# Order of the last gap and the first loads, engine of the low parts, and unread TensorE matmuls, in a layer of attention and gated feed-forward

## The chip, the cores and the metric

One core of one Trainium2 chip runs the whole program. The metric is the device time of one launch, in microseconds.

## What is computed

The input is x, 4 x 1024 x 256 in fp32. The layer is attention with 16 query heads and 4 key and value heads of width 16 (rotary positions, full softmax over 1024 keys), output projection, residual and layer norm; then a gated feed-forward of width 1024 with dequantised integer weights, residual and layer norm.

```python
q = rope((x @ wq).reshape(B, S, 16, 16)); k = rope((x @ wk).reshape(B, S, 4, 16)); v = (x @ wv).reshape(B, S, 4, 16)
scores = einsum('bqkgd,bskd->bkgqs', q.reshape(B, S, 4, 4, 16), k) / 4
x = layernorm(x + einsum('bkgqs,bskd->bqkgd', softmax(scores), v).reshape(B, S, 256) @ wo)
x = layernorm(x + (silu(x @ Wg.T) * (x @ Wu.T)) @ Wd.T)      # W = (w_int - 128) * scale
```

## The kernel before

**Stages.** The kernel is one program with an instruction list written by hand for each engine. Stage one projects x in eight blocks m of 512 positions (batch b = m // 2, half c = m % 2). Stage two is the attention, in four pairs of key heads, each of four halves of eight tiles. Stage three is the output projection and the feed-forward, with the norms. Engines wait for each other by semaphores alone.

**A block of stage one.** TensorE makes two q products (j = 0, 1) in plain fp32, each of two matmuls of 128x128 with 512 columns (`project_q`, L1179), and the k and v products (`project_kv`, L1194). VectorE multiplies the q products by cosine and sine (`rotary_q`, L706). GpSimd adds or subtracts these (`rotate`, L539). ScalarE rounds the result to its high part (`high_part`, L970), and the low part is the rest: by GpSimd (`low_of`, L547) or by VectorE (`low_first`, L726). SP stores both to q_parts in device memory (`store_q`, L380). After the second block of a batch VectorE makes the five key products (`rotary_k`, L715 and L719), GpSimd turns them (`rotate_k`, L554), and high and low parts are stored (`store_k`). In the next batch's first block `project_kv` waits for these key products, since they are read from its bank.

**Which engine takes a low part.** For j = 1 it is always GpSimd. For j = 0 it is VectorE in blocks 0 to 4 (`FIRST` is 5) and GpSimd in blocks 5 to 7. In an odd block VectorE's low part stands ahead of its key products.

**The gap.** The softmax needs a bound of the scores for each query. It comes from maxima over keys, for which three arrays are held: keys of the first half, the differences of the halves, and the "gap". TensorE makes the gap of a batch with one fp32 matmul of `key_signs` and the rotated keys (`make_gap`, L1203), ScalarE takes its high part (`gap_high`, L996) and VectorE the rest (`gap_low`, L733). SP stores both (`store_gap`, L391).

**Early work.** After FIRST blocks the maxima of the first halves start between the projections. The table `early[n, h]` says what follows hook h of block n (six hooks a block, and n = 8 after the last block): transposes of V (`transpose_v`, L1157), gaps, maxima (`max_block`, L1138, a matmul of 48 rows with 512 columns; two of a step use different rows and run side by side) and the split of the shift. TensorE, VectorE and ScalarE walk the same table, and from it a list `places` gives each entry a bank of PSUM in turn. Entries of the first kind are cut at zero by ScalarE (`difference`, L1007), and VectorE takes their maximum together with the second kind (`take_max`, L751). With n = 8, hook 1 has the V transposes of batch 3, and hook 5 has the last six steps, twelve maxima, and then the gap of batch 3.

**Loads for it.** `first_loads` on SP waits until blocks 0 and 1, keys and gap of batch 0 are stored, then issues six k_max loads (L324) and four q_sb loads (L314, L315). It stands in block 3, between the x load of block 6 (L336) and `store_q(3, 1)`. TensorE waits for them in `max_loaded(0)`, ahead of the first maxima, hook 0 of block 5.

**Start of the attention.** After the table TensorE goes to `attention`: maxima, scores (L1289) whose first banks must have been read, ScalarE's exponentials (L1062) and the products with V (`pv`, L1231), into pv_bank, which is the same bank as v_bank of stage one.

Of the kernel before, what the change touches and what calls it, by code (L numbers as in the profile page):

```python
# [6 lines left out]
B, S, E = 4, 1024, 256  # L7
# [6 lines left out]
P = 128  # L14
# [22 lines left out]
FIRST = 5  # L37
HOOKS = 6
BLOCKS = 2 * B
WARM = 3  # L40
MIXED = (0, 2, 4, 6)
PER = UNITS * G * S // P
HALVES = UNITS * QH
# [4 lines left out]
TT = CH // P  # L48
# [9 lines left out]
def layer(nc, x, xT, wq, wkv, wo, gate_w, gate_scale, up_w, up_scale, down_w, down_scale,  # L58
          cos, sin_q, cos_k, sin_k, identity, out):
    ctx = ExitStack()  # L60
    with ctx:
        def sb(name, shape, dt=fp32, scope=ctx):
            return scope.enter_context(nc.sbuf_tensor(name, shape, dt))
# [16 lines left out]
        ident = sb("ident", [P, P])  # L80
# [82 lines left out]
        k_bank, v_bank = ring_bank[2], pv_bank  # L163
# [45 lines left out]
        def paired(half, t, r):  # L209

            return KT * half + t < LEAD or (r == 0 and t in MIXED)

# [10 lines left out]
        def step(i):  # L223

            half, t = divmod(i // 2, KT)
            return [(half, 4 * t + 2 * (i % 2) + r) for r in range(GROUPS)]

        early = {(n, h): [] for n in range(BLOCKS + 1) for h in range(HOOKS)}
# [4 lines left out]
        for i in range(2 * LEAD):  # L233
            n, h = divmod(FIRST * HOOKS + i, HOOKS)
# [1 line left out]
            if i == 2 * KT + 1:  # L236
                where.append((0, "split"))
            where.extend(step(i))
        early[BLOCKS, HOOKS - 1].append(("gap", B - 1))
        for n in range(BLOCKS + 1):  # L240
            if n == BLOCKS:
                wide_from = len(readers)
# [30 lines left out]
        def taken_through(key):  # L273

            return ring_used, readers[:places[key] + 1].count("max")
# [41 lines left out]
        def load_k(dst, pair, s, done, queue):  # L317
            parts = QH + 1 if dst is k_max else QH
            head = UNITS * pair + s
            for r in range(GROUPS):  # L320
                for combo, part in enumerate((0, 0, 1)):
                    src = k_parts[head // HKV, part, 0:parts].rearrange("c (d h) t -> d h c t", h=HKV)[:, head % HKV]
                    row = r * GROUP + combo * D
                    queue.dma_start(dst[s][row:row + D].bitcast(fp32).rearrange("d (c t) -> d c t", c=parts), src).then_inc(done[s], 16)  # L324
# [4 lines left out]
        def _(sp):  # L329

            def load_kv(pair, s):
                load_k(k_sb, pair, s, kv_loaded, sp)


            def load_x(m):
                sp.dma_start(x_in[m], xT_v[:, :, m * CH:(m + 1) * CH]).then_inc(x_loaded[m], 16)  # L336
# [56 lines left out]
            def projections(b, first, last):  # L393
                for c in range(2):
                    m = 2 * b + c
                    if last and c == 0:
                        load_kv(0, 0)
                        load_k(k_max, 0, 1, kmax_loaded, sp)
                        load_q(0, QH, sp)
                    store_q(m, 0)  # L400
                    if c == 0 and not first:
                        store_gap(b - 1)
                    if m + 3 < BLOCKS:
                        load_x(m + 3)
                    if m == 3:
                        first_loads()
                    if last and c == 1:
                        load_shift(0, 0, taken_through((0, "split")))
                    store_q(m, 1)
                    if m == 4:  # L410
                        load_q(0, 1, sp)
                    if c == 1:
                        store_k(b)
# [111 lines left out]
        def _(pool):  # L525
# [36 lines left out]
            for m in range(BLOCKS):  # L562
                b, c = divmod(m, 2)
                rotate(m, 0)
                if c == 0 and b:
                    low_of_k(b - 1)
                rotate(m, 1)
                if m >= FIRST:
                    low_of(m, 0)
                low_of(m, 1)  # L570
                if c == 1:
                    rotate_k(b)
# [9 lines left out]
            for n, (w, w_h, w_l) in enumerate(((gate_w, gate_h, gate_l), (up_w, up_h, up_l), (down_w, down_h, down_l))):  # L582
                flat_h, flat_l = (t[:].rearrange("p k n -> p (k n)") for t in (w_h, w_l))
                rows = w.shape[0] // 2
                for half in range(2):
                    i = 2 * n + half
# [102 lines left out]
        def _(dve):  # L689
# [18 lines left out]
            def rotary_k(b):  # L708

                dve.wait_ge(proj_ready, 3 * (2 * b + 1) + 3)  # L710
                if b == 0:
                    dve.wait_ge(k_tables_loaded, 16 * 2)
                else:
                    dve.wait_ge(k_rot_ready, b)
                dve.tensor_tensor(by_cos[2][:], k_bank[:], cosk_sb[:], ALU.mult).then_inc(k_parts_ready, 1)  # L715
                step = HKV * HALF
                for at in range(0, P, 2 * step):
                    for to, src in ((at, at + step), (at + step, at)):
                        dve.tensor_tensor(by_sin[2][to:to + step], k_bank[src:src + step, :], sink_sb[src:src + step, :], ALU.mult).then_inc(k_parts_ready, 1)  # L719

            def low_first(m):
                b, c = divmod(m, 2)
                if b:
                    dve.wait_ge(stored[2 * c], 16 * 2 * b)
                dve.wait_ge(hi_ready, 2 * m + 1)
                dve.tensor_tensor(low[2 * c][:], rotated[0][:], high[2 * c][:].bitcast(fp32), ALU.subtract).then_inc(lo_ready[0], 1)  # L726
# [40 lines left out]
            def early_maxima(n, h):  # L767
                for key in early[n, h]:
                    if key[0] == "v":
                        continue  # L770
                    if key[0] == "gap":
                        gap_low(key[1])
                        continue
                    half, e = key
                    if e == "split":
                        split_shift(entry(key), 0, 0, None)
                        continue
                    take_max(half, e)
                    if e == MAXES - 1:
                        row_maxima(half)  # L780

            for m in range(BLOCKS):
                b, c = divmod(m, 2)
                if m == 1:
                    dve.wait_ge(ident_loaded, 16)
                    dve.tensor_tensor(key_signs[:], ident[:, 0:HKV * D], ident[:, HKV * D:P], ALU.subtract).then_inc(signs_ready, 1)
                early_maxima(m, 0)
                rotary_q(m, 0)
                early_maxima(m, 1)
                early_maxima(m, 2)  # L790
                rotary_q(m, 1)
                early_maxima(m, 3)
                early_maxima(m, 4)
                if m < FIRST:
                    low_first(m)
                if c == 1:
                    rotary_k(b)
                early_maxima(m, 5)
            for h in range(HOOKS):
                early_maxima(BLOCKS, h)  # L800
# [315 lines left out]
        def _(pe):  # L1116

            pe.wait_ge(warm_ready, 1)
            for n in range(WARM):
                pe.matmul(v_bank[:], by_cos[2][:, 0:P], by_cos[2][:], start=True, stop=True)  # L1120
            pe.wait_ge(wq_loaded, 16)

            def free_bank(key):
                pos = places[key]
                before = last_in(bank_index(pos), pos)
                if before is not None:
                    pe.wait_ge(*taken(before))
                elif wide_from <= pos < early_entries:
                    pe.wait_ge(parts_ready, Q_PARTS * BLOCKS)
                return bank_of(key)  # L1130

            def max_block(half, e):
                bank = free_bank((half, e))
                k, t = half % HALVES, e // 4
                qt, i = max_pair(t)
                r, kind = blocks(half, t)[e % 4]
                rows = slice(r * GROUP, r * GROUP + ROWS)
                pe.matmul(bank, q_sb[k][rows, i, qt * P:(qt + 1) * P], k_max[k // QH][rows, kind * CH:(kind + 1) * CH],  # L1138
                          start=True, stop=True).then_inc(ring_ready, 1)
# [13 lines left out]
            def transpose_v(b):  # L1153
# [3 lines left out]
                    ins = pe.transpose(bank[:, t * P:(t + 1) * P], v_rows[b % 2][:, t * P:(t + 1) * P], ident[:])  # L1157
                ins.then_inc(ring_ready, 1)

            def early_work(n, h):  # L1160
                for key in early[n, h]:
                    if key[0] == "v":
                        pe.wait_ge(ident_loaded, 16)
                        transpose_v(key[1])
                    elif key[0] == "gap":
                        make_gap(key[1])
                    elif key[1] == "split":
                        transpose_max(key[0])
                    else:
                        if key[1] == 0:  # L1170
                            max_loaded(key[0])
                        max_block(*key)

            def project_q(m, j, k):
                i = 2 * m + j
# [40 lines left out]
            for h in range(HOOKS):  # L1216
                early_work(BLOCKS, h)

            pe.wait_ge(parts_ready, Q_PARTS * BLOCKS)
            pe.wait_ge(k_parts_ready, K_PARTS * B)  # L1220
            pe.wait_ge(v_rows_ready, B)
# [45 lines left out]
            def attention(p, first, last):  # L1267
                for k in range(HALVES):
                    n = HALVES * p + k
                    s = k // QH  # L1270
                    for t in range(KT):
# [30 lines left out]

                        if t not in MIXED:
                            if split_at(g) is not None:
# [142 lines left out]
```

## Time and profile before

| | us |
|---|---|
| runs before, median (lowest to highest of 3) | 942.2 (941.97 to 942.79) |
| profiled execution, its own time | 944.88 |
| its span, first to last instruction | 943.1 |
| TensorE matmuls busy | 917.6 (97%) |
| VectorE busy | 756.4 (80%) |
| ScalarE busy | 715.4 (76%) |
| GpSimd busy | 247.5 (26%) |
| mean granted TensorE clock | 0.983 of full |

The profile is one execution. Its span lies 1.8 us under that execution's own time. Busy times of TensorE are modelled ends of pipelined matmuls, so full busy time is not peak work; a plain fp32 matmul appears as two records. The granted clock is a share of the full 2.4 GHz. An entry in brackets behind a row is the idle time of the engine just before it and what ended that. The stage of projections is the first tenth of the span; the rest is attention until about 700 us and then the feed-forward.

### The profile page before, as it was taken

What the parts mean: (1) busy time and instruction counts of PE and PEld (TensorE: products, weight loads), DVE (VectorE), ACT (ScalarE), POOL (GpSimd) and SP (SyncE); (2) the same over time, 40 slices, a digit from 0 to 9 for tenths busy, and PEclk for the clock granted to TensorE, in tenths of its full rate; (3) what the DMA queues carried; (4) which work ended last, traced back from release to release, by engine and by line L of the source; (5) the groups of instructions that cost most, each with busy time, mean ns of one, the idle gap of its engine ahead of it and who ended that gap; (6) DMA issues with size and microseconds to landing.
All of it is one profiled execution on the core that took longest, in us unless ns stands there. A gap on an engine that the chain in (4) does not pass through costs nothing.

```text
span 943.1 us, 15754 instructions
## 1 busy us (share of the span) xinstructions
PE 917.6 (97%) x5566; PEld 467.0 (50%) x5566; DVE 756.4 (80%) x1520; ACT 715.4 (76%) x930; POOL 247.5 (26%) x211
## 2 busy tenths in 40 slices
PE   8798999999999999999999999999999999999995
PEld 3233434344344434343434444444435888888884
DVE  5768899999999999999999999999973456655544
ACT  1345888989888898988998889988887555555564
POOL 5643565010001001001000100400101666656454
PEclk9977999999999999999999999999999999999998
DMA  7867533133131332213313123221110201101001
GB/s 251 267 182 191 126 87 94 47 79 76 44 74 43 59 75 69 51 44 75 81 44 70 50 50 81 69 55 42 32 52 15 69 23 46 46 25 43 23 23 47
DMA packets 50080, 68.78 MB, mean 73 GB/s; under 512 B 13520, under 2 KB 23760, under 8 KB 50000
## 3 DMA queue, kind: packets, MB, share of 16 engines
q1 hardware_dynamic: 49136, 64.61, 26.7%
q0 software_dynamic: 864, 3.15, 1.1%
q8 instruction: 46, 0.75, 0.3%
q14 instruction: 34, 0.28, 0.1%
HBM read 46.74 MB, written 16.25 MB: 67 GB/s over the span
## 4 chain that ended last, share of the span: by engine, by line
PE 91%; DVE 2%; ACT 2%; issue 1%; DMA 1%; POOL 1%; SPq 1%; POOLq 0%; DVEq 0%
PE pv_bank L1231 27%; PE ring_bank L1138 26%; PE pair_bank L1289 13%; PE pair_bank L1352 12%; PE pv_bank L1361 3%; PE ring_bank L1361 3%; PE ring_bank L1241 2%; PE pair_bank L1179 1%; ACT probs L1062 1%; PE pair_bank L1138 1%; PE ring_bank L1151 1%; POOL rotated L539 1%; PE ring_bank L1256 1%; DMA q_sb<-q_parts 1%; PE pv_bank L1120 1%
## 5 line engine op out<-in xcount | busy, mean ns | idle before, releaser
L1062 ACT ACTIVATE probs<-pair_bank 128x1024 f32<-128x1024 f32 x512 | 496.4, 1026 | 69.1 <-PE pair_bank L1289 67.7
L754 DVE TENSOR_REDUCE block_max<-ring_bank 128x1 f32<-128x512 f32 x732 | 469.0, 682 | 32.2 <-PE ring_bank L1138 24.2
L1138 PE MATMUL ring_bank<-k_max,q_sb 48*128 48x512 f32 x1004 | 316.0, 478 | 3.6 <-DMA q_sb<-q_parts 2.9
L1231 PE MATMUL pv_bank<-probs,v_all 128*32 128x512 f32 x2048 | 273.7, 606 | 0.6 <-ACT probs L1062 0.5
L1138 PEld LDWEIGHTS ring_bank<-k_max,q_sb 48*128 48x128 f32 x1004 | 137.0, 185 | 252.7 <-DVE block_max L754 126.0
L1289 PE MATMUL pair_bank<-q_sb,k_sb 50*128 50x512 f32 x1024 | 204.7, 416 | 1.7 <-ACT probs L1062 0.9
L617 POOL TENSOR_TENSOR attn<-attn,inv_rows 128x1024 f32<-128x1024 f32 x7 | 16.7, 2382 | 492.3 <-DMA inv_rows<-inv_d 492.3
L1289 PEld LDWEIGHTS pair_bank<-q_sb,k_sb 50*128 50x128 f32 x1024 | 101.5, 187 | 34.1 <-ACT probs L1062 14.2
L919 DVE SCALAR_TENSOR_TENSOR hid<-pair_bank,up_s,silu 128x512 f32<-128x512 f32 x64 | 47.9, 748 | 86.9 <-ACT silu L1102 86.9
L751 DVE CUSTOM_DVE_ANT_0 above<-ring_bank,above 128x512 f32<-128x512 f32 x137 | 94.4, 691 | 15.4 <-PE ring_bank L1138 6.3
L659 POOL TENSOR_TENSOR hid_l<-hid,hid_h 128x512 fp32r<-128x512 f32 x64 | 82.8, 1294 | 86.9 <-ACT hid_h L1088 86.4
L1007 ACT ACTIVATE above<-ring_bank 128x512 f32<-128x512 f32 x135 | 80.6, 599 | 7.3 <-PE ring_bank L1138 3.9
L1102 ACT ACTIVATE silu<-pair_bank,gate_s 128x512 f32<-128x512 f32 x64 | 43.7, 683 | 47.5 <-PE pair_bank L1352 47.5
L1231 PEld LDWEIGHTS pv_bank<-probs,v_all 128*32 128x32 f32 x2048 | 40.4, 108 | 74.2 <-issue 73.4
L1088 ACT ACTIVATE hid_h<-hid 128x512 fp32r<-128x512 f32 x64 | 40.3, 629 | 42.9 <-DVE hid L919 42.9
L1352 PE MATMUL pair_bank<-x1T_h,gate_h 128*128 128x512 f32 x128 | 41.0, 401 | 0.1
L1352 PE MATMUL pair_bank<-x1T_l,gate_h 128*128 128x512 f32 x128 | 40.5, 397 | 0.0
L1352 PE MATMUL pair_bank<-x1T_h,up_h 128*128 128x512 f32 x128 | 40.3, 396 | 0.0
L1352 PE MATMUL pair_bank<-x1T_l,up_h 128*128 128x512 f32 x128 | 40.3, 396 | 0.0
L1361 PE MATMUL pv_bank<-down_h,hid_h 128*128 128x256 f32 x128 | 33.7, 285 | 1.9 <-POOL hid_l L659 1.6
L1179 PE MATMUL pair_bank<-attn,wq_sb 128*128 128x512 f32 x64 | 33.6, 647 | 0.0
L1361 PE MATMUL ring_bank<-down_h,hid_h 128*128 128x256 f32 x128 | 33.5, 283 | 0.0
(128 smaller groups left out, 858.0 us busy)
## 6 DMA issues: line engine op xcount, KB each, us to landing
k_max<-k_parts SPq DMA_DIRECT2D x96, 96.0 KB, 3.5
q_sb<-q_parts SPq DMA_DIRECT2D x64, 128.0 KB, 3.5
k_sb<-k_parts SPq DMA_DIRECT2D x96, 64.0 KB, 2.3
attn<-xT SPq DMA_DIRECT2D x8, 512.0 KB, 5.3
q_parts<-high SPq DMA_DIRECT2D x16, 256.0 KB, 3.7
q_parts<-low SPq DMA_DIRECT2D x16, 256.0 KB, 3.8
q_sb<-q_parts SPq DMA_DIRECT2D x64, 64.0 KB, 3.6
attn<-pv_sb SPq DMA_DIRECT2D x128, 32.0 KB
```

The source lines that it names most:

```text
L659: pool.tensor_tensor(hid_l[:, it, :], hid[it % 2][:], hid_h[:, it, :].bitcast(fp32), ALU.subtract).then_inc(hid_l_ready, 1)
L751: dve.tensor_tensor_reduce(out=buf[:], in0=bank, in1=buf[:], scale=1.0, scalar=-3.0e38, op0=ALU.add, op1=ALU.max, accum_out=block_max[half ...
L754: dve.reduce_max(block_max[half % 2][:, col:col + 1], bank, axis=AX.X).then_inc(ring_used, 1)
L919: dve.scalar_tensor_tensor(out=hid[it % 2][:], in0=pair_bank[it % 2][:, 1, :], scalar=up_s[:, it:it + 1], in1=silu[it % 2][:], op0=ALU.mul ...
L1007: act.activation(above[(count - 1) % 2][:], bank_of(key), ACT.Relu).then_inc(above_ready, 1)
L1062: act.activation(probs[t % 2][:, 2 * pr:2 * pr + 2, :], pair_bank[pr][:], ACT.Exp, scale=D ** -0.5).then_inc(probs_ready, 1)
L1102: act.activation(silu[it % 2][:], pair_bank[it % 2][:, 0, :], ACT.Silu, scale=gate_s[:, it:it + 1]).then_inc(silu_ready, 1)
L1138: pe.matmul(bank, q_sb[k][rows, i, qt * P:(qt + 1) * P], k_max[k // QH][rows, kind * CH:(kind + 1) * CH], start=True, stop=True).then_inc( ...
L1231: ins = pe.matmul(pv_bank[32 * j:32 * j + 2 * D, :], v_all[:, head, t, :], probs[t % 2][:, 2 * (j % 2) + j // 2, :], start=(t == 0), stop= ...
L1289: ins = pe.matmul(pair_bank[pr][:, r, :], k_sb[s][rows, t * P:(t + 1) * P], q_sb[k][rows, pr, :], start=True, stop=True)
L1352: ins = pe.matmul(pair_bank[it % 2][:, u, :], w[:, k, it * P:(it + 1) * P], v[c][:, k, :], start=(q == 0), stop=(q == len(terms) - 1))
L1361: ins = pe.matmul(sum_bank[t // 2][:, (t % 2) * E:(t % 2 + 1) * E], v[:, k, t * P:(t + 1) * P], w[:, k, :], start=(k == 0 and t % 2 == 0 a ...
```

## The change

Five edits, all ahead of the attention. The gap of batch 3 moves in the table from the end of hook 5 of n = 8 to hook 4, so on TensorE, ScalarE and VectorE it stands ahead of the last twelve maxima. SP calls `first_loads` in block 2. The low parts (j = 0) of blocks 1 and 3 go from VectorE to GpSimd. In block 4 and the other even ones nothing changes. TensorE gets matmuls of the identity by itself, fp32, 128 columns each, whose results nobody reads: 16 into the first maxima's bank ahead of the wait for the first loads, one into v_bank after each of the twelve maxima of n = 8, and 8 ahead of the waits before the attention.

```diff
@@ -38,6 +38,7 @@
 WARM = 3
+FIRST_BUSY, LAST_BUSY = 16, 8
@@ -236,7 +237,7 @@
             where.extend(step(i))
-        early[BLOCKS, HOOKS - 1].append(("gap", B - 1))
+        early[BLOCKS, HOOKS - 2].append(("gap", B - 1))
@@ -402,7 +403,7 @@
                         load_x(m + 3)
-                    if m == 3:
+                    if m == 2:
                         first_loads()
@@ -565,7 +566,7 @@
                 rotate(m, 1)
-                if m >= FIRST:
+                if c == 1 or m >= FIRST:
                     low_of(m, 0)
                 low_of(m, 1)
@@ -791,10 +792,10 @@
                 early_maxima(m, 4)
-                if m < FIRST:
-                    low_first(m)
                 if c == 1:
                     rotary_k(b)
+                elif m < FIRST:
+                    low_first(m)
                 early_maxima(m, 5)
@@ -1157,6 +1158,11 @@
+            def keep_busy(bank, count):
+
+                for i in range(count):
+                    pe.matmul(bank[:, (i % TT) * P:(i % TT + 1) * P], ident[:], ident[:], start=True, stop=True)
+
@@ -1167,9 +1173,13 @@
                     else:
+                        if key == (0, 0):
+                            keep_busy(free_bank(key), FIRST_BUSY)
                         if key[1] == 0:
                             max_loaded(key[0])
                         max_block(*key)
+                        if n == BLOCKS:
+                            keep_busy(v_bank, 1)
@@ -1216,6 +1226,7 @@
                 early_work(BLOCKS, h)
 
+            keep_busy(v_bank, LAST_BUSY)
             pe.wait_ge(parts_ready, Q_PARTS * BLOCKS)
```

## Rows read from the trace of the kernel before

**Rows 1.** Stretches: length; PE, PEld, DVE, ACT, POOL busy; PE clock; DMA share; GB/s.

```profile
20.00:40.00 20.00, 14.77 (x48) 5.15 (x48) 16.17 (x25) 5.74 (x12) 12.58 (x10) 1.00 0.81 253
46.00:51.00 5.00, 4.92 (x12) 2.08 (x12) 0.99 (x3) 1.74 (x4) 0.16 (x1) 0.66 0.93 279
60.00:68.00 8.00, 8.00 (x19) 2.21 (x18) 4.28 (x11) 2.09 (x4) 4.54 (x4) 0.57 0.21 76
80.00:98.50 18.50, 16.60 (x55) 7.83 (x59) 13.83 (x34) 11.45 (x19) 4.58 (x4) 0.54 0.55 164
120.00:680.00 560.00, 560.00 (x3656) 226.74 (x3653) 524.24 (x1001) 500.33 (x594) 50.35 (x31) 1.00 0.27 63
```

**Rows 2.** TensorE in order of time: start, duration, work [idle before].

```profile
23.77 0.64 PE L1194 MATMUL ring_bank<-attn,wkv_sb 128*64 128x512 f32 x1 [2.92 <-DVE by_sin L719]
...
25.54 1.02 PE L1203 MATMUL ring_bank<-rotated_k,key_signs 128*64 128x512 f32 x2
...
38.44 0.64 PE L1194 MATMUL ring_bank<-attn,wkv_sb 128*64 128x512 f32 x1 [2.31 <-DVE by_sin L719]
...
46.08 0.49 PE L1138 MATMUL ring_bank<-k_max,q_sb 48*128 48x512 f32 x2 [2.94 <-DMA q_sb<-q_parts]
...
58.61 0.49 PE L1138 MATMUL pair_bank<-k_max,q_sb 48*128 48x512 f32 x1 [1.19 <-DVE block_max L751]
```

**Rows 3.** VectorE, then GpSimd, then TensorE, in order of time, end of the projections.

```profile
78.97 2.84 DVE L719 TENSOR_TENSOR by_sin<-ring_bank,sink_sb 32x512 f32<-32x512 f32 x4
...
81.89 1.27 POOL L554 TENSOR_TENSOR rotated_k<-by_cos,by_sin 128x512 f32<-128x512 f32 x1 [0.64 <-DVE by_sin L719]
...
80.43 0.69 PE L1157 MATMUL pair_bank<-ident,v_rows 128*128 128x128 f32 x4 [0.55 <-issue]
...
86.64 1.97 PE L1203 MATMUL pair_bank<-rotated_k,key_signs 128*64 128x512 f32 x2
...
90.15 0.79 PE L1289 MATMUL pair_bank<-q_sb,k_sb 50*128 50x512 f32 x2 [0.82 <-DVE gap_l L733]
...
98.33 1.07 PE L1231 MATMUL pv_bank<-probs,v_all 128*32 128x512 f32 x8
```

**Rows 4.** VectorE in order of time, block 1.

```profile
19.16 1.08 DVE L726 TENSOR_TENSOR low<-rotated,high 128x512 fp32r<-128x512 f32 x1 [1.44 <-ACT high L970]
20.17 0.68 DVE L715 TENSOR_TENSOR by_cos<-ring_bank,cosk_sb 128x512 f32<-128x512 f32 x1
20.88 2.84 DVE L719 TENSOR_TENSOR by_sin<-ring_bank,sink_sb 32x512 f32<-32x512 f32 x4
```

**Rows 5.** GpSimd in order of time, block 1.

```profile
17.20 2.50 POOL L539 TENSOR_TENSOR rotated<-by_cos,by_sin 128x512 f32<-128x512 f32 x2 [1.96 <-DVE by_sin L706]
20.43 1.26 POOL L547 TENSOR_TENSOR low<-rotated,high 128x512 fp32r<-128x512 f32 x1 [0.74 <-ACT high L970]
23.80 1.27 POOL L554 TENSOR_TENSOR rotated_k<-by_cos,by_sin 128x512 f32<-128x512 f32 x1 [2.10 <-DVE by_sin L719]
```

**Rows 6.** SP's issues (gap_l, x of block 6, first loads); then landing of gap_l.

```profile
31.23 0.59 SPq L391 DMA_DIRECT2D k_parts<-gap_l  x1
...
35.50 0.74 SPq L336 DMA_DIRECT2D attn<-xT  x1
36.51 3.09 SPq L324 DMA_DIRECT2D k_max<-k_parts  x6
...
41.04 0.43 SPq L315 DMA_DIRECT2D q_sb<-q_parts  x1
...
DMA to landing us min/median/max: 2.9/3.5/4.0
```

**Rows 7.** The chain that ended last: start, us, what.

```profile
67.63 0.85 PE ring_bank L1203 x2
...
72.98 0.44 PE ring_bank L1157 x4
```

**Rows 8.** ScalarE in order of time, first exponentials.

```profile
90.98 1.94 ACT L1062 ACTIVATE probs<-pair_bank 128x1024 f32<-128x1024 f32 x2 [1.02 <-PE pair_bank L1289]
```

## The prediction

> **What bounds the kernel now.** I read the table of stretches first. From 120 to 680 us TensorE is busy in all of the 560 us at full clock [rows 1]: this is the attention, and whatever lets it start sooner ends the program sooner by as much, while nothing in the change touches its inside. So only the first 100 us matter. There the same table shows three spells at the lower granted clock (half, 1.2 instead of 2.4 GHz): the means 0.66 over 5 us, 0.57 over 8 us and 0.54 over 18.5 us are spells of 5 x 0.34 x 2 = 3.4 us, 8 x 0.43 x 2 = 6.9 us and 18.5 x 0.46 x 2 = 17 us. TensorE is busy nearly throughout all three, so each costs up to half its length.
>
> Then TensorE in order of time [rows 2]. In block 2 it idles 2.92 us and in block 4 2.31 us until VectorE has made the key products; at the first maxima (block 5) it idles 2.94 us until 46.08, for q_sb to land. It had arrived at 46.08 - 2.94 = 43.14. The first slow spell follows right on this, the second on an idle of 1.19 us at 57.4, behind VectorE. In block 2 the idle of 2.92 us brought no fall (20 to 40 us: 1.00 [rows 1]): an idle gap between maxima is worse than a longer one between projections.
>
> Last, the end of the stage [rows 3]. VectorE ends the last key products at 78.97 + 2.84 = 81.81, call it K. GpSimd turns them at 81.89 to 83.16. TensorE meanwhile transposes V (80.43), runs the twelve last maxima, makes the gap at 86.64 and starts the first scores at 90.15 (K + 8.3) when gap_l is done; its second pv starts at 98.33 (K + 16.5), from where the steady pace holds. Except for the first instants all of it is at half clock.
>
> **Part 1: low parts of odd blocks on GpSimd.** Blocks 1 and 3 drop one VectorE subtraction ahead of the key products. In block 1 VectorE waits 1.44 us for ScalarE, subtracts for 1.08 us and begins the key products at 20.17 [rows 4]. Without both it begins at 20.17 - 2.46 = 17.7 and ends at 17.7 + 0.7 + 2.84 = 21.25 instead of 23.72. TensorE's wait ends there too: 21.3 for 23.77. GpSimd has the rotations until 19.70, then both low parts, 1.26 us each, to 22.2, then the rotated keys to 23.45; before they ended at 25.07 [rows 5]. The gap matmul of block 2, at 25.54 before, waits for it: 23.5, so 2.0 us gained and 0.4 us of the new GpSimd work shown. Block 3 the same way: VectorE goes from the q products straight to the key products, and the two gains add up; I get key products done at 33.9, TensorE just through with the q projections of block 4, so its wait of 2.31 us is gone and it stands at 34.0 where it stood at 38.44. It arrives at the first maxima at 43.14 - 4.4 = 38.8. Here a page speaks against the edit. The rows: the same subtraction is 1.08 us on VectorE and 1.26 on GpSimd. GPSIMD Engine Reference of the Trainium skill, section 3.1, has an elementwise op of two operands 1.96 times slower on GpSimd; by it the move would take 2.1 us a block, and the estimate by that page would be 0.9 us less gain in block 2. The row decides.
>
> **Part 2: first loads one block sooner.** SP issued gap_l of block 0 at 31.23 and the first loads from 36.51 to 41.5 [rows 6]. Gap_l comes 2.3 us sooner by part 1, issued at about 28.9; it lands 2.9 to 4.0 us later (same group), and now SP stands and waits for it, until about 32.4. Ten issues take the 5.0 us that they take now, the last at about 36.9. Before, it landed 5.0 us after its issue, with stores and an x load in the queues ahead of it; now less is ahead: 3.5 (the middle of gap_l's) to 5.0, so 40.4 to 41.9. Queued behind on SP are the second store of block 2 (now at 37.4 and 38.0, landing some 4 us later, by 42), then block 3's stores and the x load of block 6, at 39.6 instead of 35.50; block 6 begins after 48. ScalarE's high part of block 4 waits for that store: some 2 us, and with it the first two relus, which follow it, by under 1 us; VectorE takes those 2 us after the maxima, so this costs 0 to 0.6, taken as nothing.
>
> **Part 3: sixteen identity matmuls before the first maxima.** No such matmul is in the trace. Four transposes with the same shapes go in 0.44 us, and a plain fp32 matmul of 512 columns in 0.85 [rows 7], so 128 columns are 0.21 to 0.28 us; I take 0.22. Sixteen are 3.5 us (to 4.5): 38.8 + 3.5 = 42.3. The loads land under it. The first maxima move from 46.08 to 42.3: **3.8 us gained** (2.8 to 4.1). The idle that preceded the first spell is filled, so the spell's half of 3.4 us is saved: **1.7 us** (0 if the clock falls anyway).
>
> **Part 4: gap first, fillers, then attention.** The projections of block 7 and K are unchanged in order. TensorE is done with the V transposes at 80.43 + 0.69 [rows 3], K - 0.7, and now idles 2 us for the rotated keys, until K + 1.35, with nothing in it: the fillers stand behind the maxima. At full clock: gap 0.85 [rows 7]; twelve maxima that ran in pairs (a pair 0.49, the next start a little sooner [rows 2]) now each stand between fillers that use every row, so 12 x (0.43 + 0.22) = 7.8; the last eight fillers 1.8: K + 11.8. Then 0.4 of maxima, scores at K + 12.2. VectorE has six readings there, each about as long as its products of 0.68 [rows 4], and stays under cover; its last is done within the eight fillers. From the scores the first four exponentials set the pace, 0.97 us each (two in 1.94 [rows 8]): with the scores and hand-overs 4.4 us to the second pv, K + 16.6, against K + 16.5 before. What the higher clock gives, the broken pairs, the fillers and the wait take: **0.1 us lost**. But the idle of 2 us among maxima and transposes will, by rows 1 and 2, bring a fall about K. How long it lasts after the gap starts is the unknown. Nothing if it does not fall; 3.4 us if it goes as the first spell, which ended under dense projections; 6.9 as the second; 17 as the third, which ended only in the attention. The fillers are nearest to the first: **1.7 us lost** (0 to 3.4, 7 in the rival below).
>
> The sum: -3.8 - 1.7 + 0.1 + 1.7 = -3.7 us. It is made against the profiled execution (span 943.1, own time 944.88, 2.7 above the median of the runs, 942.2) and taken off the median: **938.5 us**.
>
> **The rivals.** *Second spell goes too.* It follows a stall of 1.19 us in which maxima wait for VectorE at the key products; the change does nothing to it, so it should stay, but it comes earlier and after a stretch without a spell. If it goes, half of 6.9: 938.5 - 3.4 = 935.1.
>
> *The clock never falls at the end.* The fillers then do it all: 938.5 - 1.7 = 936.8, with the second spell gone too 933.4. TensorE: Matmul & The Clock Gate of the Trainium skill, Part 1, holds that throttled is the default and activity releases it; by that rule fillers behind the gap bring the clock back, but the idle ahead of it stays unfilled. Here the trace agrees, with a spell after each idle between maxima.
>
> *Given back.* The first maxima are not earlier, as gap_l lands late or SP's delayed stores hold ScalarE: 2 us less there, and a second-spell length (3.4 us lost) at the end: 938.5 + 2 + 1.7 = 942.2, no change.
>
> *Slower: the fillers run at half clock.* The clock falls in the idle before the gap and returns only in the attention, as the third spell did. Then gap, maxima and fillers take double, 10.4 us more, and the ramp the 8.2 us seen (90.15 to 98.33) for 4.4, 3.8 more: 14.2 instead of 1.7, so 942.2 - 5.4 + 14.2 = 951.0. It decides from the point where half of the slow time exceeds the gain of 5.4: 10.8 us of half clock after the gap starts. For it: the third spell is 17 us with TensorE busy in most of it. Against: its maxima ran without dense matmuls between them.
>
> **How the numbers follow.** Forecast 0.40; second spell gone 0.22; no fall at the end 0.15; given back 0.13; slower 0.10. A measurement here can tell 0.2%, 1.9 us. Faster by more (under 940.3) are the first three: 0.77. Same 0.13, slower 0.10. The range runs from just under the all-fast case, 933.0, over the forecast's unknowns (fillers of 0.28 on the path: 36 x 0.06 = 2.2; a spell of 6.9 at the end: 1.7) to 942.2; above it lie the slower case and half of the one given back, 0.16.
>
> **What would show it.** Part 1: gap of block 2 at 23.5, no idle in block 4. Part 2 and 3: fillers from 38.8, first maxima at 42.3, q_sb landed before. Clock 1.00 from 40 to 50; a spell of about 7 us somewhere in 50 to 62. K at about 76.3; then 2 us of idle, gap, fillers at 0.22 (0.44 while slow), scores at K + 12 to 16, second pv at K + 16.6 plus half the slow time. The forecast is wrong if the first maxima are later than 43.5, if K does not move with them, or if the scores start later than K + 16.

## The result, and the profile after

| | before | after |
|---|---|---|
| median (lowest to highest of 4 runs) | 942.09 us (941.45 to 942.79) | 952.76 us (952.01 to 953.45) |
| profiled execution, its own time | 944.88 | 953.45 |
| its span | 943.1 | 951.6 |
| mean granted TensorE clock | 0.983 | 0.980 |

The changed kernel is slower: the ratio is 1.0100, with a 95% interval of 1.0073 to 1.0126. The forecast was 938.5 us with a range to 942.2; the time lies above it, and the sign is wrong. It is near the rival called slower (951.0).

The head of the page of the changed kernel: span, TensorE's busy tenths in 40 slices, and the granted clock in the same slices.

```profile
span 951.6 us, 15898 instructions
...
PE   9998999999999999999999999999999999999995
...
PEclk9995899999999999999999999999999999999998
```

TensorE is fuller than before (98%), its clock lower in the fourth slice (71 to 95 us). The stage of projections in order of time, first TensorE up to the second slow spell, then VectorE's last key products [rows 2, 3]. In this kernel L1204 is `project_kv`, L1213 `make_gap`, L1164 the identity matmuls, L1139 the maxima.

```profile
22.89 1.02 PE L1213 MATMUL ring_bank<-rotated_k,key_signs 128*64 128x512 f32 x2
...
33.52 0.64 PE L1204 MATMUL ring_bank<-attn,wkv_sb 128*64 128x512 f32 x1
...
38.35 3.73 PE L1164 MATMUL ring_bank<-ident 128*128 128x128 f32 x32
42.01 0.50 PE L1139 MATMUL ring_bank<-k_max,q_sb 48*128 48x512 f32 x2
...
53.02 0.50 PE L1139 MATMUL pair_bank<-k_max,q_sb 48*128 48x512 f32 x1 [1.20 <-DVE block_max L752]
```

```profile
71.86 2.84 DVE L720 TENSOR_TENSOR by_sin<-ring_bank,sink_sb 32x512 f32<-32x512 f32 x4
```

The early part of the prediction comes out: the key and value matmuls of block 4 follow without idle, the sixteen identity matmuls (32 records) start at 38.35, the first maxima at 42.01 instead of 46.08, and the last key products end at 71.86 + 2.84 = 74.70 instead of 81.81. So 7.1 us are gained by then. Then TensorE from the V transposes to the second pv:

```profile
73.32 0.63 PE L1158 MATMUL pair_bank<-ident,v_rows 128*128 128x128 f32 x4 [0.56 <-issue]
76.14 1.94 PE L1213 MATMUL pair_bank<-rotated_k,key_signs 128*64 128x512 f32 x2 [2.19 <-issue]
78.01 0.79 PE L1139 MATMUL pair_bank<-k_max,q_sb 48*128 48x512 f32 x1
78.73 0.79 PE L1164 MATMUL pv_bank<-ident 128*128 128x128 f32 x2
79.46 0.79 PE L1139 MATMUL ring_bank<-k_max,q_sb 48*128 48x512 f32 x1
80.18 0.80 PE L1164 MATMUL pv_bank<-ident 128*128 128x128 f32 x2
...
94.65 4.06 PE L1164 MATMUL pv_bank<-ident 128*128 128x128 f32 x18
98.64 0.50 PE L1139 MATMUL ring_bank<-k_max,q_sb 48*128 48x512 f32 x2
...
106.58 1.06 PE L1242 MATMUL pv_bank<-probs,v_all 128*32 128x512 f32 x8
```

A filler is here an identity matmul whose result nobody reads. The rows left out are steps like 78.01 to 79.46, all alike: 0.72 us from a maximum to its filler and 0.72 from the filler to the next maximum, 1.445 a step. The twelfth maximum starts at 93.92, its filler and the last eight (18 records) at 94.65. The attention's first maxima start at 98.64 and the second pv at 106.58, against 98.33 before [rows 3]: what was 7.1 us sooner is 8.25 later. The granted clock by stretches [rows 1]:

```profile
40.00:51.00 11.00, 11.00 (x51) 5.15 (x49) 6.90 (x16) 6.07 (x12) 5.39 (x5) 1.00 1.00 326
51.00:60.00 9.00, 7.80 (x21) 2.28 (x21) 6.77 (x15) 3.02 (x6) 3.72 (x4) 0.81 0.72 234
73.00:100.00 27.00, 24.48 (x67) 14.34 (x67) 9.07 (x24) 6.40 (x13) 9.42 (x7) 0.56 0.58 161
100.00:107.00 7.00, 6.67 (x30) 2.70 (x34) 5.19 (x11) 5.17 (x7) 3.60 (x3) 0.76 0.25 75
```

There is no spell at the first maxima. The second spell is (1 - 0.81) x 2 x 9 = 3.4 us where it was 6.9. The third is (1 - 0.56) x 2 x 27 = 23.8 us, with TensorE busy in all of it but the idle ahead of the gap, and one of 3.4 us more follows in the first tiles of the attention.

### The profile page after: what moved, and what is told of

Same layout as the page of the kernel before. It is cut to its first block, busy times and chain, and to the rows that moved or that the text cites. A ratio compares the mean times of both kernels' runs of the same rounds, so it can differ in the third digit from the quotient of the medians.

```text
span 951.6 us, 15898 instructions
## 1 busy us (share of the span) xinstructions
PE 932.8 (98%) x5638; PEld 479.0 (50%) x5638; DVE 753.9 (79%) x1518; ACT 715.0 (75%) x930; POOL 249.3 (26%) x213
## 4 chain that ended last, share of the span: by engine, by line
PE 94%; DVE 2%; ACT 2%; issue 1%; DMA 0%; SPq 0%; POOL 0%; POOLq 0%; DVEq 0%
PE pv_bank L1242 26%; PE ring_bank L1139 25%; PE pair_bank L1300 13%; PE pair_bank L1363 11%; PE pair_bank L1189 3%; PE pv_bank L1372 3%; PE ring_bank L1372 3%; PE ring_bank L1252 2%; PE pv_bank L1164 1%; PE pair_bank L1139 1%; PE ring_bank L1204 1%; ACT probs L1063 1%; PE pv_bank L1204 1%; PE ring_bank L1152 1%; PE ring_bank L1267 1%
## 5 line engine op out<-in xcount | busy, mean ns | idle before, releaser
L1139 PE MATMUL ring_bank<-k_max,q_sb 48*128 48x512 f32 x1004 | 314.5, 475 | 0.4 <-DVE block_max L752 0.2
L1139 PEld LDWEIGHTS ring_bank<-k_max,q_sb 48*128 48x128 f32 x1004 | 136.0, 184 | 247.5 <-DVE block_max L755 127.6
L1242 PEld LDWEIGHTS pv_bank<-probs,v_all 128*32 128x32 f32 x2048 | 40.4, 108 | 73.6 <-issue 72.8
L1372 PE MATMUL pv_bank<-down_h,hid_l 128*128 128x256 f32 x128 | 33.3, 281 | 0.0
```

Of the source, the lines that this page charges most:

```text
L1242: ins = pe.matmul(pv_bank[32 * j:32 * j + 2 * D, :], v_all[:, head, t, :], probs[t % 2][:, 2 * (j % 2) + j // 2, :], start=(t == 0), stop= ...
L1372: ins = pe.matmul(sum_bank[t // 2][:, (t % 2) * E:(t % 2 + 1) * E], v[:, k, t * P:(t + 1) * P], w[:, k, :], start=(k == 0 and t % 2 == 0 a ...
```

## The experiments

The kernels ran in four groups, each with the kernel before beside it on the same chip. There the kernel before had medians of 942.9 to 943.3 us and single runs from 940.1 to 948.4. Each execution has its spells of half clock at somewhat other times, so single profiles differ, and ratios with their intervals decide. All times below are medians; "K" is the end of the last key products. An example of the scatter: e4_gap_alone is the kernel before in everything up to K, and its profile has K at 77.65 and no second spell, where the kernel before has 81.81 and one of 6.9 us. How much of the 7.1 us above is gain can't be told from the two profiles alone.

| kernel | us | ratio to before (95%) |
|---|---|---|
| e1_no_between | 940.67 | 0.9968 (0.9950 to 0.9986) |
| e2_gap_last | 949.00 | 1.0068 (1.0046 to 1.0091) |
| e3_early_only | 941.11 | 0.9977 (0.9964 to 0.9990) |
| e4_gap_alone | 944.63 | 1.0012 (0.9989 to 1.0035) |
| e5_fill_gap_wait | 942.37 | 1.0000 (0.9977 to 1.0023) |
| e6_no_first | 938.49 | 0.9956 (0.9934 to 0.9978) |
| e7_last_only | 940.18 | 0.9969 (0.9954 to 0.9984) |
| e9_fillers_moved | 944.54 | 1.0014 (0.9999 to 1.0029) |
| e10_low_alone | 943.65 | 1.0002 (0.9990 to 1.0015) |
| e11_loads_alone | 941.47 | 0.9980 (0.9961 to 0.9999) |
| e12_no_first_last | 940.11 | 0.9973 (0.9957 to 0.9989) |
| e13_fillers_full_clock | 944.23 (one run) | not taken |
| e14_fillers_by_pairs | 947.30 | 1.0048 (1.0030 to 1.0066) |
| e15_no_first_again | 938.34 | 0.9956 (0.9941 to 0.9970) |
| e16_early_only_again | 941.31 | 0.9990 (0.9973 to 1.0007) |

### The twelve fillers or the gap put first

Two theories of the loss: F, the twelve identity matmuls between the last maxima; G, the gap put first, with its idle and the spell.

```diff
# e1_no_between, against the changed kernel
-                        if n == BLOCKS:
-                            keep_busy(v_bank, 1)
# e2_gap_last, against the changed kernel
-        early[BLOCKS, HOOKS - 2].append(("gap", B - 1))
+        early[BLOCKS, HOOKS - 1].append(("gap", B - 1))
# e4_gap_alone, against the kernel before
-        early[BLOCKS, HOOKS - 1].append(("gap", B - 1))
+        early[BLOCKS, HOOKS - 2].append(("gap", B - 1))
```

> The changed kernel without the twelve single identity matmuls between the last maxima; gap order and the other fillers stay. Theory F (the loss is the fillers between the maxima: a maximum and a filler take 1.445 us at half clock where a maximum of a pair took some 0.5): gap at 76.1, the twelve maxima in about 6 us, last fillers 3.5, second pv at about 96 instead of 106.6; time 942.1 - 2.3 = about 940 us. Theory G (the loss is the gap put first, with its idle of 2.2 us and the spell it brings): the time stays above that of the kernel before, 946 or more.

> The changed kernel with the gap of batch 3 back behind the last maxima; all three sorts of fillers stay. Theory F: the twelve maxima and fillers start some 2 us sooner, at 74, and if the clock is still half they take 17 us again; time 949 to 952. Theory G: the idle ahead of the gap and the spell are gone, maxima and fillers run at full clock in about 8 us, second pv at about 92, time 937 or less.

> The kernel before with only the gap of batch 3 put ahead of the last maxima, no filler anywhere. Theory F: the gap starts at 83.2 at half clock, 1.9 us, then the maxima in about 6 us, scores at about 91.5 where they were at 90.15: 1.3 us slower, 943.4. Theory G: 946 or more.

Without the twelve fillers the changed kernel goes from 1.0100 to 0.9968 of the kernel before, some 12 us. With the gap back at its place but the fillers kept it stays at 1.0068. The gap moved alone gives 1.0012, not told from nothing; F had 1.3 us slower. e1_no_between and e7_last_only (below) differ in the place of the gap alone, and have 0.9968 and 0.9969; e2_gap_last and e7_last_only differ in the twelve fillers alone, and are 9 us apart. So F holds and G falls; beside the twelve fillers the gap put first may cost some 3 us, with intervals that overlap. In the profile of e2_gap_last the idle ahead of the gap is gone, and yet the stretch has its spell, of (1 - 0.53) x 2 x 22 = 20.7 us with TensorE busy in all 22 us:

```profile
73.00:95.00 22.00, 22.00 (x56) 12.52 (x58) 7.33 (x20) 5.35 (x10) 2.67 (x3) 0.53 0.43 126
```

So the half clock comes and stays without the idle ahead of the gap; idles of 0.2 to 0.55 us do stand ahead of this spell, and no run removes those alone.

### The same number of fillers in other places

```diff
# e9_fillers_moved: no filler between the maxima, and
-FIRST_BUSY, LAST_BUSY = 16, 8
+FIRST_BUSY, LAST_BUSY = 16, 20
# e14_fillers_by_pairs
-                        if n == BLOCKS:
-                            keep_busy(v_bank, 1)
+                        if n == BLOCKS and key[1] % 2:
+                            keep_busy(v_bank, 2)
```

> The changed kernel with the same number of identity matmuls, but the twelve that stood one behind each of the last maxima now stand in one row with the last eight (twenty ahead of the attention). Theory A (what costs is where they stand: alternation exposes weight loads, breaks the pairs and does not bring the clock back): the twenty take 5 to 9 us in a row and the clock returns under them; about 943, at most 945, some 8 us better than the changed kernel. Theory B (the number of fillers costs): 950 or more.

> The changed kernel with the same twelve fillers among the last maxima, but two behind each pair, so that the two maxima of a step stand next to each other again. If the broken pairs are the cost: a step (two maxima, two fillers) takes about 1.9 us at half clock instead of 2.89, six steps 6 us less, and about 946.5. If the shown weight loads at each change are: half of the changes are left, 2.3 us a step and 949. If it is the number of fillers: no gain, 952.

All 36 identity matmuls are in both kernels. In a row ahead of the attention the twelve cost about 4 us: 944.54 against 940.67 of e1_no_between, which lacks them. Singly between the maxima they cost 12: the changed kernel is 8 us above e9_fillers_moved. TensorE in order of time, e9_fillers_moved and then e14_fillers_by_pairs:

```profile
77.00 1.94 PE L1211 MATMUL pair_bank<-rotated_k,key_signs 128*64 128x512 f32 x2 [2.20 <-issue]
78.87 0.79 PE L1139 MATMUL pair_bank<-k_max,q_sb 48*128 48x512 f32 x1
...
81.88 1.40 PE L1139 MATMUL pair_bank<-k_max,q_sb 48*128 48x512 f32 x2
83.21 6.47 PE L1164 MATMUL pv_bank<-ident 128*128 128x128 f32 x40
89.61 0.50 PE L1139 MATMUL ring_bank<-k_max,q_sb 48*128 48x512 f32 x2
```

```profile
79.97 0.79 PE L1139 MATMUL pair_bank<-k_max,q_sb 48*128 48x512 f32 x1
...
80.69 1.22 PE L1164 MATMUL pv_bank<-ident 128*128 128x128 f32 x4
81.84 0.79 PE L1139 MATMUL pair_bank<-k_max,q_sb 48*128 48x512 f32 x1
...
90.06 3.70 PE L1164 MATMUL pv_bank<-ident 128*128 128x128 f32 x20
93.69 0.50 PE L1139 MATMUL ring_bank<-k_max,q_sb 48*128 48x512 f32 x2
```

The twelve maxima of e9_fillers_moved take 83.21 - 78.87 = 4.3 us at half clock, as pairs that also overlap each other, and the twenty fillers 6.4 us, the clock returning at about 86.9 within them. With pairs kept and two fillers behind each, a step takes 81.84 - 79.97 = 1.87 us where the changed kernel takes 2 x 1.445 = 2.89: six steps are 6.1 us less, and 947.3 is 5.5 less than the changed kernel. Of the 1.02 us of a step, 0.72 are the two maxima, which run side by side again (79.97 to 80.69), and 0.29 the two fillers, which now stand together (1.15 us for 1.44). Broken pairs are thus 4.3 us, about half of the 8 us between the changed kernel and e9_fillers_moved. The 3 us left between e14_fillers_by_pairs and e9_fillers_moved fit what their rows show, pairs of different steps that no longer overlap and a clock that returns at 92.6 instead of 86.9; no run parts the two.

### What one filler costs

```diff
# e13_fillers_full_clock: low parts and loads as in the changed kernel,
# gap at the end, no other filler; in block 7
+                        if n == BLOCKS - 1:
+                            keep_busy(free_bank(key), 1)
                         max_block(*key)
```

> Low parts and first loads sooner, and one identity matmul ahead of each of block 7's twelve maxima, where the clock was full; no others. If alternation exposes the weight loads at full clock too, a maximum and its filler take about 0.72 us (half of the 1.445 at half clock), 12 of them 8.7 where the pairs took 2.6, so the last key products come 5 to 6 us later and the time is 943 to 945. If it is a matter of the half clock alone, 0.43 + 0.22: 5 us or less more in sum, last key products 4 to 5 us later. If fillers between maxima hold the clock, no spell begins in this block or at its end.

```profile
62.37 0.49 PE L1139 MATMUL pair_bank<-k_max,q_sb 48*128 48x512 f32 x1
62.79 0.49 PE L1164 MATMUL ring_bank<-ident 128*128 128x128 f32 x2
63.21 0.49 PE L1139 MATMUL ring_bank<-k_max,q_sb 48*128 48x512 f32 x1
63.63 1.13 PE L1187 MATMUL pair_bank<-attn,wq_sb 128*128 128x512 f32 x2
```

```profile
57.00:80.00 23.00, 22.63 (x83) 10.55 (x83) 15.30 (x37) 11.15 (x22) 11.23 (x10) 1.00 0.63 153
```

At full clock a maximum takes 0.42 us and so does a filler beside it (62.79 to 63.21 to 63.63), while sixteen in a row took 3.66 us, 0.23 each. An identity matmul behind a maximum costs nearly two of a row, at full clock as at half: 0.42 and 0.72 against 0.23 and 0.44. The 0.19 more at full clock is as long as one of its weight loads (0.192 us by the profile of the changed kernel), and the 0.28 more at half is as long as the shortest of them there (0.287), so a load that nothing hides is the likely reason; that is argued from the durations, no run isolates it. The expectation was off in the size: with the first maxima at the same time (39.24, in e15_no_first_again 39.32) K is 3.6 us later, not 4 to 6. The clock stays full until 80.3 here, 3.7 us behind K; in the other profiles with the early parts it fell at 72.6 to 77.8, and in none more than 1.1 us behind K. So the single fillers may have put the fall off, but they did not prevent it: a spell of 20.5 us follows, as long as in e15_no_first_again, and the one run is 944.23.

### Fillers in a row, and the clock

```diff
# e3_early_only: no fillers after the projections, gap at the end
# e7_last_only: the same, with the eight ahead of the attention
+            keep_busy(v_bank, LAST_BUSY)
# e5_fill_gap_wait: gap first; only this in the last stage
                     elif key[0] == "gap":
+                        if n == BLOCKS:
+                            keep_busy(v_bank, 12)
                         make_gap(key[1])
```

> The changed kernel with only its early parts: low parts on GpSimd, first loads one block sooner, sixteen fillers ahead of the first maxima. Gap at the end, no fillers after the projections. The last key products are done at 74.70 in the changed kernel and at 81.81 before, 7.1 us sooner. If the end of the stage then runs as before, second pv at 91.2 and time 942.1 - 7.1 = 935.0 us. Rival: the clock falls at another place of the stage and takes 2 to 3 us of it back, 937 to 938.

> The early parts with the gap at the end, plus only the eight fillers ahead of the attention. Theory A (fillers in a row bring the clock back): the spell that ended at 97.5 without them ends by about 88, the eight cost 2 to 3.5 us and the ten saved us of half clock give back up to 5; 938.5 to 941. If fillers in a row do not matter to the clock, they only cost: 943 to 944.

> The changed kernel with the fillers of the last stage replaced by twelve in a row in the idle of 2.2 us ahead of the gap; none between the maxima, none ahead of the attention. If a dense row in the idle holds or soon restores the clock: spell under 7 us, second pv 15 us after the last key products, 936 to 938. If the clock falls all the same and stays until the attention: spell 17 us or more, 941 to 943.

Granted clock from before the last spell to after it, for e3_early_only, e7_last_only and e5_fill_gap_wait:

```profile
72.00:99.00 27.00, 25.18 (x92) 10.81 (x92) 18.96 (x43) 16.27 (x23) 10.92 (x8) 0.56 0.58 163
```

```profile
77.00:86.00 9.00, 8.49 (x30) 4.92 (x30) 6.14 (x19) 4.51 (x8) 2.34 (x2) 0.62 0.63 194
```

```profile
74.00:93.00 19.00, 16.74 (x73) 9.89 (x71) 12.48 (x31) 10.53 (x17) 3.73 (x4) 0.73 0.64 188
```

Without late fillers the spell is (1 - 0.56) x 2 x 27 = 23.8 us and reaches to 97.5, well into the attention: that is part of why e3_early_only has 941.1 instead of the 935.0 expected. Its second pv is at 90.18, 8.1 us sooner than before, but the next two follow 3.9 us apart, where the steady pace is some 2.5: 2.9 us given back there. What else parts the profile's gain from the median's is not followed. In e7_last_only, with the eight in a row (83.46 to 86.0), the spell is (1 - 0.62) x 2 x 9 = 6.8 us and ends at 84.6, under them. In the changed kernel, in e2_gap_last, e9_fillers_moved, e12_no_first_last and e14_fillers_by_pairs it ended under this row as well, in e1_no_between 1.2 us behind it. They cost about what they bring: 0.9969 against 0.9977 and 0.9990 of the kernels without them. Twelve in the wait for the gap shortened the profiled spells to 3.4 and 6.8 us, but at half clock the row runs to 78.4 and holds the gap back 2 us; the median is no better than before, and its expectation of 936 to 938 is missed. The profile is of an execution of 940.13, one of five from 938.0 to 940.7; the other five took 944.0 to 945.6, at a lower mean clock (0.981 to 0.985 instead of 0.988 to 0.990), and no profile shows where their spells lie.

### The early parts

```diff
# e10_low_alone: the kernel before with low_of(m, 0) for c == 1 on GpSimd
# e11_loads_alone: the kernel before with
-                    if m == 3:
+                    if m == 2:
                         first_loads()
# e6_no_first, e15_no_first_again: both of these, and no filler anywhere
# e16_early_only_again: e3_early_only again
# e12_no_first_last: e6_no_first with the last eight
```

> The kernel before with only the low parts of blocks 1 and 3 on GpSimd. By the prediction's steps TensorE arrives at the first maxima 4.4 us sooner (38.8), but the loads, still issued in block 3 after its stores, land only about 2 us sooner than 46.08, at 43 to 44: last key products 2 to 3 us sooner, 940 to 941 us. If the low parts are worth nothing without the loads: 942 to 943.

> The kernel before with only the first loads one block sooner. TensorE arrives at 43.1 as before and the loads have landed by about 43: the idle of 2.94 us nearly goes, and perhaps the first spell with it: 938 to 940 us. If SP's later stores hold ScalarE instead: 942 or more.

> The early parts without the sixteen fillers ahead of the first maxima: low parts on GpSimd and first loads sooner alone. TensorE arrives at the first maxima at 38.4 and the loads land at about 40: idle of some 2 us, then maxima 2 us sooner than with the fillers. If the fillers were what kept the clock there, a spell of 3.4 us follows and costs 1.7: the same as with them, 941. If the idle brings no spell: 939.

> Low parts and first loads sooner, no fillers ahead of the first maxima, gap at the end, and only the eight fillers in a row ahead of the attention. If the two findings add (no first fillers: 2 us better; last eight: the spell ends under them for about their own price): 937 to 939. If the first fillers are what makes the last ones pay: 940 or more.

> Same kernel as e6_no_first (low parts on GpSimd and first loads one block sooner, nothing else), against the kernel before again: 938.5, between 937.5 and 940.

> Same kernel as e3_early_only, which has the sixteen fillers ahead of the first maxima besides: if they cost what their place on TensorE's path says (3.7 us of fillers over an idle of 1.3 to 1.8), 2 us more than the run beside it, 940.5 to 941. If the difference was between the chips: the same as beside it.

TensorE at the first maxima, e10_low_alone and then e6_no_first, and the clock of both:

```profile
44.47 0.80 PE L1138 MATMUL ring_bank<-k_max,q_sb 48*128 48x512 f32 x2 [5.78 <-DMA q_sb<-q_parts]
...
40.00:59.00 19.00, 14.53 (x31) 4.83 (x32) 7.77 (x16) 5.58 (x12) 5.38 (x5) 0.55 0.75 228
```

```profile
40.78 0.50 PE L1139 MATMUL ring_bank<-k_max,q_sb 48*128 48x512 f32 x2 [1.84 <-DMA q_sb<-q_parts]
...
38.00:52.00 14.00, 11.21 (x36) 3.67 (x34) 10.02 (x19) 6.54 (x14) 8.17 (x7) 1.00 0.91 282
```

The low parts alone bring TensorE to the maxima sooner only to wait there: 5.78 us, and in that execution a spell of 17 us begins in the wait (mean clock 0.55). No gain, where 2 us had been expected. The loads alone give 1.8 us. Both together give 4.4 to 5.0: TensorE waits 1.84 us, and no spell stands at that place, nor in e12_no_first_last, e13_fillers_full_clock and e15_no_first_again with waits of 1.27 to 1.62; the kernel before, e4_gap_alone and e10_low_alone, with 2.94, 3.06 and 5.78, each had one. The sixteen fillers are longer (3.66 us) than this wait, and what they were to prevent does not come without them: side by side, 938.34 without and 941.31 with them. The last eight did not add to this (e12_no_first_last, 940.11), so its expectation of a sum is missed.

The low parts and the loads alone, e15_no_first_again, are the best version that ran: 0.9956 (0.9941 to 0.9970) of the kernel before, 5.0 us less, and some 14 less than the changed kernel.

## Why the prediction was wrong

**Parts 1 and 2, right.** Gap of block 2 at 22.89 (said 23.5), block 4 without idle at 33.52 (34.0), fillers from 38.35 (38.8). SP waited for gap_l and issued the first loads at 31.58, and in e6_no_first q_sb has landed at 40.78 (40.4 to 41.9), in three others at 39.1 to 39.3. ScalarE's high part of block 4 did wait for SP's delayed store, 4.5 us and until 42.34 where some 2 had been said, and in the changed kernel TensorE shows no idle behind it. Without the sixteen fillers it does: ahead of the second pair of maxima TensorE waits 0.4 to 0.7 us for ScalarE's delayed relu (e6_no_first, e12_no_first_last, e15_no_first_again), about the 0 to 0.6 us that the prediction allowed and took as nothing.

**Part 3, right in its sum, wrong in its reason.** First maxima at 42.01 (42.3), no spell: 4.1 us and 1.7. But the reason given, that the fillers save the spell, falls with e6_no_first. The wait itself had shrunk to 1.84 us and brought none. The fillers end later than the loads land, 42.3 against 40.4 to 41.9 in the prediction's own numbers, and this difference was not weighed as a price; e16_early_only_again has its first maxima 2.8 us later than e15_no_first_again (42.11, 39.32), and the median is 3 us higher.

**The second spell** was forecast to stay and was half as long, which with the rest made K 7.1 us sooner instead of 5.5. This lies within the scatter, so this part of the gain was luck of the execution: the profiles of the other kernels have 0, 3.4 or 6.8 us at this place, and e4_gap_alone, the same code up to there as the kernel before, has none.

**Part 4, where it failed.** Two steps. The first: "fillers are nearest to the first spell: 1.7 us lost". The spell lasted 23.8 us and ended only behind the last maximum, under the row of eight. The choice rested on likeness, a dense fp32 matmul as in the projections; yet a single identity matmul between two maxima is not a stretch of projections, and nothing in rows 1 had it. The second: the filler at 0.22 us, a quarter of the 0.85 of a gap matmul [rows 7] (the four transposes in 0.44 are 0.11 each and don't give it). That price holds in a row. Alone between maxima it is 0.42 at full clock and 0.72 at half, and the maximum beside it is 0.72 at half too. From K to the second pv the prediction had 16.6 at full clock and it took 31.9. The 15.3 more are: gap 1.0; twelve steps 12 x (1.445 - 0.65) = 9.5, of which 2.3 are the filler's price (0.84 for 0.65 at full clock) and the rest the half clock; the last row, 95.37 to 98.64 against 1.8, 1.5; scores to second pv 7.6 against 4.4, 3.2. With the 7.1 us gained at K this gives the 8.25 later; the own times of the two profiled executions differ by 8.6 and the medians by 10.7, since the one of the kernel before was 2.8 above its median and the other 0.7.

**The rivals.** The slower one named this mechanism and its price well, 14.2 us for the measured 15.3, and its time, 951.0, is 1.8 under the median. That it came so close is partly luck: it doubled a filler of 0.22 to 0.44 where 0.72 was measured, and took a ramp of 8.2 us where 7.6 was measured. It had a chance of 0.10. The evidence for it was at hand, and the prediction named it: the third spell before was 17 us with TensorE busy in most of it, just where the fillers were to stand. The range ended at 942.2 and did not reach it. TensorE: Matmul & The Clock Gate of the Trainium skill, Part 1, has it that activity releases the throttle. The rows of eight and twenty, under which the clock returned, agree. The alternation does not: by the profile TensorE is busy without a break from 76.14 to 94.65, and the clock stays at half. Here the measurement decides.

## What to carry to other kernels

A filler is free only in time that nobody else needs: keep it in a row, not between matmuls that run side by side, and price it at half clock as well as at full, since the last twelve here ran at half. A known idle stretch is no guarantee: twelve in the wait of 2.2 us ran 2 us over and gained nothing. Where TensorE waits, try first to shorten the wait; the two edits that did so, alone, are worth 5 us here, and no filler that was added to them paid. Two edits that feed one wait must be made together: low parts alone only moved TensorE's idle, loads alone gave about a third.

## What was not expected of the hardware

- An identity matmul of 128 columns took 0.23 us in a row and 0.42 behind a maximum at full clock, 0.44 and 0.72 at half.
- Half clock stayed over 18 us of unbroken busy time with maxima and identity matmuls in turn (e2_gap_last: all of 22 us busy, mean clock 0.53), and ended under rows of eight to twenty identity matmuls in six kernels; in a seventh, e1_no_between, it ended 1.2 us behind the row.
- After such a return the first tiles of the attention could bring another spell (3.4 us in the changed kernel, 6.8 in e9_fillers_moved and e5_fill_gap_wait), so not all of what a row of fillers gives back is kept.
- The place of the spells differs from execution to execution: the kernel before has runs of 940.1 to 948.4 us. Why a spell of the same code is 3.4 us in one and 6.8 in another stays open.
